# Attention groups of small matmul tiles set apart by whole products, two homes for two value tiles, another order for gates and exponentials

## What is computed

```
mod = (silu(c) @ wmod).reshape(2, 6, 1, 256); sa, ca, ga, sb, cb, gb = mod parts
h = layernorm(x) * (1 + ca) + sa
x = x + ga * gated_linear_attention(h)      # 16 heads of 16, chunks of 64 tokens
h = layernorm(x) * (1 + cb) + sb
x = x + gb * moe(h)                         # 8 experts, best 2 of them, width 176; a shared one, width 704

# attention, for each chunk: G = cumsum(log_sigmoid(h Wg1 Wg2 + bg2) / 16)
qg = Q * scale * exp(G);  o_inter = qg @ S
A  = tril((Q * exp(G - G0) * scale) @ (K * exp(G0 - G)).T);  o_intra = A @ V
S  = S * exp(Glast) + (K * exp(Glast - G)).T @ V
o  = rms_norm(o) * norm_w * silu(h Wgate);  out = o @ Wo
```

## Time and profile before

| | us |
|---|---|
| runs | 387.04, 387.41, 384.47 |
| median | 387.04 |
| profiled execution | 386.04 |
| its span | 384.2 |
| slot 1 (first gate product to first gate product) | 40.6 to 75.0 |
| slot 2 | 75.0 to 115.6 |
| slot 3 (to the first scores of slot 4) | 115.6 to 148.5 |
| slot 4, to the end of its mean squares | 148.5 to 174.0 |
| rest of the shared expert, sorting | 174 to 257 |
| expert tiles, combination | 257 to 384 |

### The profile page before, as it was taken

The page is one execution under the profiler, slowest core; times in us unless marked ns, Lnnn a source line. Parts: engine busy times, 40 slices in busy tenths (PEclk is TensorE's granted clock), DMA queues, the critical chain, the costliest instruction groups (busy, mean ns, idle before and its releaser), DMA issues.

```text
span 384.2 us, 9939 instructions
## 1 busy us (share of the span) xinstructions
PE 359.4 (94%) x3837; PEld 224.8 (59%) x3838; DVE 239.4 (62%) x578; ACT 144.4 (38%) x303; POOL 146.2 (38%) x252
## 2 busy tenths in 40 slices
PE   2989989997989899699999999999999999999996
PEld 2445655674556556554864564576666666666464
DVE  3068767796778878945286483236555555555386
ACT  3395718642846350335023311113333333332110
POOL 7504203500240062005544046540667777675300
PEclk9999999998999999999999999999999999999999
DMA  7960300000000000039931045242233333311296
GB/s 251 309 201 2 114 3 3 2 5 3 1 2 3 3 2 3 4 114 333 292 101 62 1 113 136 90 140 57 83 112 100 108 102 98 99 56 43 83 352 229
DMA packets 29901, 36.66 MB, mean 95 GB/s; under 512 B 4567, under 2 KB 26530, under 8 KB 29860
## 3 DMA queue, kind: packets, MB, share of 16 engines
q1 hardware_dynamic: 26452, 27.58, 23.9%
q0 software_dynamic: 3408, 8.51, 6.5%
HBM read 23.31 MB, written 13.68 MB: 96 GB/s over the span
## 4 chain that ended last, share of the span: by engine, by line
PE 85%; ACT 6%; DVE 4%; issue 3%; DMA 1%; SPq 0%; DVEq 0%; ACTq 0%
PE at_ps L1815 13%; PE work L1445 10%; PE at_ps L1445 8%; PE work L1494 6%; PE at_ps L1460 6%; PE work L1838 4%; PE work L1460 3%; PE work L1840 3%; PE work L1681 2%; PE work L1631 2%; PE at_ps L1494 2%; PE at_ps L1799 2%; PE at_ps L1528 2%; PE at_ps L1681 2%; PE o_even L1584 1%
## 5 line engine op out<-in xcount | busy, mean ns | idle before, releaser
L656 POOL DMA_INDIRECT ys_tokens<-er_pos,goal_u x39 | 41.8, 1073 | 33.8 <-DVE er_pos L1368 25.6
L1815 PE MATMUL at_ps<-arena 128*128 x156 | 54.5, 472 | 0.0
L627 POOL DMA_INDIRECT xs_sorted<-h2tok,pos_u x32 | 31.8, 993 | 36.9 <-DVE pos_u L992 18.6
L585 POOL TENSOR_TENSOR sq<-sq,sg 128x512 f32<-128x512 f32 x8 | 10.0, 1271 | 92.6 <-issue 92.6
L1815 PEld LDWEIGHTS at_ps<-arena 128*128 128x128 f32 x156 | 26.6, 190 | 14.9 <-issue 6.6
L898 ACT ACTIVATE arena<-at_ps 128x176 f32<-128x176 f32 x39 | 12.4, 317 | 58.8 <-PE at_ps L1815 58.8
L1368 DVE SCALAR_TENSOR_TENSOR er_pos<-work,goal,sq 128x256 f32<-128x256 f32 x39 | 17.2, 480 | 22.0 <-PE work L1845 21.0
L1445 PE MATMUL work<-h2T,sup_sb 128*128 128x512 f32 x56 | 25.7, 598 | 0.0
L1348 DVE TENSOR_TENSOR arena<-at_ps,arena 128x176 f32<-128x176 f32 x39 | 13.3, 341 | 18.4 <-ACT arena L898 15.9
L1195 DVE COPY_PREDICATED arena<-causal,at_ps 128x512 f32<-128x512 uint32 x32 | 20.5, 719 | 5.8 <-PE at_ps L1528 5.8
L1460 PE MATMUL at_ps<-sdn_sb,hs 128*128 128x256 f32 x100 | 22.1, 380 | 0.0
(11 more groups left out here) (281 smaller groups left out, 815.6 us busy)
## 6 DMA issues: line engine op xcount, KB each, us to landing
h2tok<-xs_sorted SPq DMA_DIRECT2D x40, 131.5 KB, 2.1
arena<-ys_tokens SPq DMA_DIRECT2D x8, 512.0 KB, 7.8
arena<-in_e_up SPq DMA_DIRECT2D x8, 352.0 KB, 5.5
x_sb<-in_x SPq DMA_DIRECT2D x4, 512.0 KB, 6.9
out_rows<-x_sb SPq DMA_DIRECT2D x16, 128.0 KB, 4.2
sup_sb<-in_s_up SPq DMA_DIRECT2D x2, 640.0 KB, 4.7
xs_sorted<-state SPq DMA_DIRECT2D x2, 526.0 KB, 15.2
xs_sorted<-state SPq DMA_DIRECT2D x8, 131.5 KB, 3.8
```

The lines of the kernel that those rows point to most:

```text
L627: g.indirect_dma_start(out=xs_dram, out_offset=bass.IndirectOffsetOnAxis(ap=pos_u[:, k, t:t + 1], axis=0), in_=h2tok[:, t, :], in_offset=N ...
L656: g.indirect_dma_start(out=ys_dram, out_offset=bass.IndirectOffsetOnAxis(ap=goal_u[:, i:i + 1], axis=0), in_=yout[:, q % 2, u, :], in_offs ...
L1815: ins = t_.matmul(at_ps[2 + u % 2][:, 0:2 * FE], xT[:, u % 2, k * P:(k + 1) * P], eup[:, bass.ds(e, 1), k, :].rearrange("p a n -> p (a n)" ...
```

## The change

TensorE, slots 1 to 3: `values(s, 0)` moves up between `scores_first` and `from_state`; K of half 0 between `from_state` and `scores_second`; the first of the two h2 transposes between `scores_second` and the first `from_chunk`; K of half 1 between the two `from_chunk`, with a wait for the mask that frees its bank; the second transpose, `mean_squares` and then `router` come behind the second `from_chunk`, and `logits_by_token` between the two query products. In slot 4 the shared part "half" stands in front of `scores_second`, and "second" in front of the second `from_chunk`.

The value tiles 0 and 1 of odd blocks get a second home, `vpad_odd` (zeroed once on GpSimd); ScalarE no longer waits for `from_chunk` ahead of `evac_v(s, 0)`. The masks are applied in the order of banks 2, 3, 0, 1 (`MASK_ORDER`). VectorE runs `log_gate(s, 0)` ahead of the masks and the x statistics ahead of the key evacuations. ScalarE takes er_neg out of `gate_exps` (`gate_neg`), one half behind `evac_v`, the other behind the first transpose's evacuation; `rstd_of(1)` goes behind the silu of G, and the squares ahead of the second transpose's evacuation, er_pos and the router's.

```diff
...
-BANKS = {("G", 0): 0, ("G", 1): 1, ("V", 0): 0, ("HT", 0): 1, ("HT", 1): 0, ("K", 0): 1, ("RT", 0): 0, ("RX", 0): 0, ("K", 1): 2,
+BANKS = {("G", 0): 0, ("G", 1): 1, ("V", 0): 0, ("HT", 0): 0, ("HT", 1): 0, ("K", 0): 1, ("RT", 0): 0, ("RX", 0): 0, ("K", 1): 2,
          ("Q", 0): 3, ("Q", 1): 1, ("V", 1): 0, ("KT", 0): 2, ("KT", 1): 3, ("XT", 0): 1, ("XT", 1): 0, ("WO", 0): 2,
...
+MASK_ORDER = (2, 3, 0, 1)
...
         put("V", s, 0)
+        put("K", s, 0)
         if h >= 0:
             put("HT", h, 0)
+        put("K", s, 1)
+        if h >= 0:
             put("HT", h, 1)
-        put("K", s, 0)
+            put("RT", h, 0)
+        put("Q", s, 0)
         if h >= 0:
-            put("RT", h, 0)
-        for kind, j in (("K", 1), ("Q", 0), ("Q", 1), ("V", 1), ("KT", 0), ("KT", 1)):
+            put("RX", h, 0)
+        for kind, j in (("Q", 1), ("V", 1), ("KT", 0), ("KT", 1)):
             put(kind, s, j)
-            if (kind, j) == ("K", 1) and h >= 0:
-                put("RX", h, 0)
         if s + 1 < NBLK:
...
     fill(NBLK, "gates")
+    fill(NBLK, "half")
     turn(("HT", NBLK - 2, 0), ("HT", NBLK - 2, 1), ("RT", NBLK - 2, 0))
-    fill(NBLK, "half")
+    fill(NBLK, "second")
     turn(("RX", NBLK - 2, 0), ("RK", 0, 0))
-    fill(NBLK, "second")
     ring.append(4)
...
         atm = part(2 * NPAIR * 512).rearrange("p (a j n) -> p a j n", a=2, j=NPAIR)
+        vpad_odd = part(2 * KC * NPAIR * 64).rearrange("p (t r w) -> p t r w", t=2, r=KC * NPAIR)
         wmod_sb = hs[:, :, :].rearrange("p f n -> p (f n)").rearrange("p (k n) -> p k n", k=KC)
...
+        def v_rows(s, t):
+            return vpad_odd[:, t] if t < 2 and s % 2 else vpad[:, t]
...
                             ALU.mult).then_inc(const_pool, 1)
+            steps.did(g.memset(vpad_odd, 0.0))
+            steps.sync()
             g.memset(vpad, 0.0).then_inc(zero_ready, 1)
...
-            def evac_h2T(b):
-                for k in range(KC):
+            def evac_h2T(b, ks=range(KC)):
+                for k in ks:
                     wait_unit(act, ("HT", b, k))
...
                 for t in range(2):
-                    ins = a.activation(free_dims(vpad[:, 2 * jj + t, 0, 0:1], [[64, KC * NPAIR], [48, 2], [1, HEAD]]),
+                    ins = a.activation(free_dims(v_rows(s, 2 * jj + t)[:, 0, 0:1], [[64, KC * NPAIR], [48, 2], [1, HEAD]]),
                                        bank(("V", s, jj))[:, t * HID:(t + 1) * HID]
...
+            def gate_neg(s, gr):
+                act.wait_ge(r_ready, 2 * s + gr + 1)
+                if s >= 1 and gr == 0:
+                    act.wait_ge(qeo_ready, 4 * s)
+                a.activation(er_neg[:, gr, :], gk[:, gr, :], ACT.Exp, scale=-1.0 / GATE_NORM).then_inc(neg_ready, 1)
             def gate_exps(s):
-                for gr in range(KC):
-                    act.wait_ge(r_ready, 2 * s + gr + 1)
-                    if s >= 1 and gr == 0:
-                        act.wait_ge(qeo_ready, 4 * s)
-                    a.activation(er_neg[:, gr, :], gk[:, gr, :], ACT.Exp, scale=-1.0 / GATE_NORM).then_inc(neg_ready, 1)
                 for gr in range(KC):
...
                     softplus(s)
-                if h >= 0:
+                else:
                     rstd_of(1, h + 1, h)
...
                 if s < NBLK:
-                    if b >= 0:
-                        act.wait_ge(set_used, 2 * b + 1)
-                    else:
+                    if h >= 0:
+                        rstd_of(1, h + 1, h)
+                    if b < 0:
                         act.wait_ge(zero_ready, 5)
                     evac_v(s, 0)
-                if h >= 0:
+                    gate_neg(s, 0)
+                    if h >= 0:
+                        evac_h2T(h, (0,))
+                    gate_neg(s, 1)
+                    if b >= 0:
+                        out_squares(b)
+                    if h >= 0:
+                        evac_h2T(h, (1,))
+                    gate_exps(s)
+                    if h >= 0:
+                        evac_router(h)
+                else:
+                    fill(s, "half")
                     evac_h2T(h)
                     evac_router(h)
-                fill(s, "half")
-                if b >= 0:
+                    fill(s, "second")
                     out_squares(b)
-                fill(s, "second")
                 if fills:
                     exp_ln_tables()
-                if s < NBLK:
-                    gate_exps(s)
                 if s + 1 < NBLK:
...
                     dve.wait_ge(set_used, n - 1)
-                for j in range(NPAIR):
+                for j in MASK_ORDER:
                     dve.wait_ge(at_full, NPAIR * n + j + 1)
...
                     ln_stats(1, h * TPB)
+                if s < NBLK:
+                    log_gate(s, 0)
                 if b >= 0:
...
                     mask_scores(2 * b)
+                fill(s, "gates")
                 if h >= 0:
                     h2_rows(h)
-                fill(s, "gates")
+                fill(s, "half")
                 if b >= 0:
                     mask_scores(2 * b + 1)
-                if s < NBLK:
-                    log_gate(s, 0)
-                else:
+                if s == NBLK:
                     steps.did(v.tensor_copy(iota_f[:, :], iota_i[:, :]))
...
                     pick_experts(dve, v, steps, 0)
-                fill(s, "half")
+                fill(s, "second")
                 if s < NBLK:
...
                     copy_ranks(dve, v, 0, bank(("RK", 0, 0)))
-                fill(s, "second")
                 if s == NBLK:
...
                     token_weights(dve, v, steps, 0)
+                if s + 1 < NBLK:
+                    dve.wait_ge(ld_x[s + 1], 16)
+                    ln_stats(0, (s + 1) * TPB)
                 if s < NBLK:
...
                         v.tensor_tensor(kh[:, gr, :], bank(("K", s, gr))[:, :], er_neg[:, gr, :], ALU.mult).then_inc(kh_ready, 1)
-                if s + 1 < NBLK:
-                    dve.wait_ge(ld_x[s + 1], 16)
-                    ln_stats(0, (s + 1) * TPB)
                 if h >= 0 and s < NBLK:
...
                         if b >= 1 and q == 0:
-                            pe.wait_ge(atm_ready, NPAIR * (2 * b - 1) + j + 1)
+                            pe.wait_ge(atm_ready, NPAIR * (2 * b - 1) + MASK_ORDER.index(j) + 1)
                         score(2 * b, q, j)
...
                         if q == 0:
-                            pe.wait_ge(atm_ready, NPAIR * 2 * b + j + 1)
+                            pe.wait_ge(atm_ready, NPAIR * 2 * b + MASK_ORDER.index(j) + 1)
                         score(2 * b + 1, q, j)
...
                                     ins = t_.matmul(o_ps[e][32 * j:32 * j + 32, o_reg(gr, t)],
-                                                    vpad[ks, t, gr * NPAIR + j, 32 * h:32 * h + 32],
+                                                    v_rows(b, t)[ks, gr * NPAIR + j, 32 * h:32 * h + 32],
                                                     atm[ks, n % 2, j, q:q + CHUNK],
...
-            def transpose_h2(b):
+            def transpose_h2(b, ks=range(KC)):
                 pe.wait_ge(h2tok_ready, b + 1)
-                for k in range(KC):
+                for k in ks:
                     o = begin(("HT", b, k))
...
                             ins = t_.matmul(at_ps[e][r, reg], ktok[ks, t, gr, r],
-                                            free_dims(vpad[ks, t, gr * NPAIR + j, 0:1], [[48, 2], [1, HEAD]]),
+                                            free_dims(v_rows(s, t)[ks, gr * NPAIR + j, 0:1], [[48, 2], [1, HEAD]]),
                                             start=True, stop=True)
...
                     scores_first(b)
+                if s < NBLK:
+                    if s == 0:
+                        pe.wait_ge(ld_wv, 16)
+                    values(s, 0)
                 fill(s, "gates")
...
                     if s == 0:
-                        pe.wait_ge(ld_wv, 16)
-                    values(s, 0)
+                        pe.wait_ge(ld_wk, 16)
+                    project(("K", s, 0), wk_sb, 0, hT)
+                fill(s, "half")
                 if b >= 0:
                     scores_second(b)
+                if h >= 0:
+                    transpose_h2(h, range(KC) if s == NBLK else (0,))
+                if b >= 0:
                     from_chunk(b, 2 * b)
-                if h >= 0:
-                    transpose_h2(h)
-                if s < NBLK:
-                    if s == 0:
-                        pe.wait_ge(ld_wk, 16)
-                    project(("K", s, 0), wk_sb, 0, hT)
-                if h >= 0:
+                if s == NBLK:
+                    router(h)
+                    fill(s, "second")
+                else:
+                    if b >= 0:
+                        pe.wait_ge(atm_ready, NPAIR * (2 * b + 1) + MASK_ORDER.index(2) + 1)
+                    project(("K", s, 1), wk_sb, 1, hT)
+                if b >= 0:
```

(30 more changed lines are left out.)

## The result

The changed kernel takes 383.42 us (median of 10 runs, 381.91 to 384.59); the kernel before, on the same chip, 387.23 us (10 runs, 384.47 to 388.11). The ratio is 0.9914, 95% interval 0.9889 to 0.9938: 3.3 us or 0.9% faster. That is within 1% and inside the forecast range, but by only 0.2 us (its lower end is 383.2); the forecast itself was 0.7 us faster, 386.3. The profiled execution took 383.4 us (span 381.6), where the one of before took 386.04.

The account below looks back on a forecast made before the run. TensorE, busy 94% of the span, bounds the kernel, with slot stalls from instruction fetch. Slots 1 to 4 sum +1.4 - 1.8 + 1.4 - 1.7 = -0.7 us, giving 386.3 us; range 383.2 to 389.8.

Parts of the forecast that it names:

- Slot 1: +1.4 us: gate-bank wait +0.45, stall where `scores_second` and `from_chunk` still touch 1.8 for 1.45, mean squares waiting +0.6.
- Slot 3: +1.4 us: h2 transpose waits 1.1 us for VectorE; output product waits 1.7 us for yT instead of 0.81.
- What is late next: Slot 3, VectorE: `evac_logits` and `top_two` (1.25 us) lose their cover ahead of the query evacuations; `gated_out` ends 144.7, was 143.34.
- Slot 4: -1.7 us: `from_chunk` stall of 1.40 and router wait of 0.7 go; SiLU bank wait of 0.25 comes.
- 3.4 to 3.9 us: TensorE's instruction fetch: a block of 256 instructions comes this long after the border before it was passed.
- Slot 2: -1.8 us, middle of -2.6 (stall, half clock and yT wait go) and -1.0 (1.6 us of stall return).
- the walk: TensorE's queue followed with old-trace pitches, each group waiting for its needs; slot 2's query product at 96.65, y at 105.5.
- the prediction's signs: Signs to look for in the trace, among them output products of slots 2 and 3 waiting 1.2 to 1.8 us for yT.
- (A): Rival: fetch problem really goes, slots 1 and 2 lose their stalls; -3.3 us, 383.7 us; chance 0.18.
- (B): Rival: waits for h2 bring the clock down in slots 2 and 3, stall in full; +2.7, 389.8 us; chance 0.14.
- (C): Rival: tile-shape switches cost 0.4 us instead of 0.1 at 8 islands; +2.4 over forecast, 388.7 us; chance 0.05.
- (D): Rival: every 256 instructions have a border, stalls only change place, sum zero; 387.0 us; chance 0.63 together with the forecast.

Follow-up runs that it names:

- run with the rows first: Changed kernel with VectorE taking the first log gate behind the expert-input rows instead of ahead of the masks in slots 2 and 3: 384.44 us, ratio 0.9936.
- shift of 136: Changed kernel with 136 idle instructions, as 34 small products, at the head of TensorE's program: 381.15 us, ratio 0.9853; made of waits instead, 391.01 us.
- first shifted run: Kernel before with 200 more instructions, waits on a long-set semaphore, at the head of TensorE's program: 405.93 us, ratio 1.0493.
- cheap shift of 168: Kernel before with 168 instructions, as 42 small identity products, at the head of TensorE's program: 388.40 us, ratio 1.0033.

## Why the prediction was right or wrong

**Slot 1, right.** Forecast +1.4, measured +1.8. The border at 1217 stayed inside the pair that still touches, as the prediction said, with 1.70 us (forecast 1.8); the value product waits 0.5 us for the gate (0.45), the mean squares 0.7 us for the squares (0.6). Not foreseen: 0.44 us at the next border, which is the difference.

```profile
54.77 0.26 PE L1605 MATMUL o_odd<-arena 64*32 64x64 f32 x3 [1.70 <-issue]
```

**Slot 3, right.** Forecast +1.4, measured +1.0. The rows of the second norm are late by 0.9 us (1.1). "What is late next" is in the trace as walked; the rows of the changed kernel that answer to the earlier trace rows are

```profile
136.92 0.20 DVE L1168 COPY logits<-work 128x36 f32<-128x36 f32 x1 [4.80 <-PE work L1638]
138.12 1.39 DVE L1329 SCALAR_TENSOR_TENSOR arena<-at_ps,qsel,er_pos 128x512 f32<-128x512 f32 x2
...
141.76 0.68 DVE L1235 TENSOR_TENSOR yT<-o_odd,sq 128x512 f32<-128x512 f32 x1
```

yT ends 28.7 us after the slot's first gate product, where the forecast had 144.7 - 115.6 = 29.1, and the output product waits 1.3 us (1.7). What the prediction could not see is that moving the top two out of this chain gives 0.9 us at most, with intervals that overlap.

**Slot 4, right.** Forecast -1.7, measured -1.9: the 1.40 us stall and the router's wait of 0.7 went, 0.6 us in the state products and 0.5 us for the SiLU (0.25) are left. The "3.4 to 3.9 us" from border to block does not hold for the stall in the state products: it was 5.9 us in before and is 6.0 now. Five instructions behind the border (148.86 us) TensorE's sequencer waits from 149.76 us for the state that GpSimd writes,

```profile
150.69 0.67 POOL L623 TENSOR_TENSOR arena<-state,tmask 128x64 f32<-128x64 f32 x1
```

and the packet starts at 152.56 us, 1.2 us after the state is there; in before it is 1.2 us as well. The shared part's products run over this wait, so it shows in no list of waits, only in the stall behind. That this wait is what held the packet is read from the times and was not tested alone.

**Slot 2, the step that failed.** The prediction let 0.8 us of the old stall stand, as the middle between none and 1.6, because "the fetch of the block ... starts only when the sequencer is some 30 instructions past a border, and the wait for h2 stands in front of that point". All queues together moved this in 86 to 90 us, in forty slices of 0.1, with the wait's end beside it:

```profile
GB/s 0 0 0 0 0 0 0 0 0 0 0 0 0 0 0 0 0 0 0 0 0 164 0 0 0 0 0 0 0 0 0 0 0 0 0 0 0 0 0 0
```

```profile
88.85 0.66 PE L1623 MATMUL work<-ident,h2tok 128*128 128x128 f32 x4 [0.99 <-DVE h2tok L1226]
...
90.89 1.56 PE L1515 MATMUL at_ps<-hT,wk_sb 128*128 128x512 f32 x3
```

The block's packet starts at 88.1 to 88.2 us, 0.7 us ahead of the end of the wait (88.85). The border (instruction 2497) stands 11 instructions ahead of the waiting transpose, and 11 were enough. So this wait did not block the fetch; it covered it. The prediction's rule was not wrong altogether, as slot 4 shows, where a wait 3 to 5 instructions behind the border goes with a late packet; what failed is its 30 instructions. The chunk product behind runs through the border at 2753 without a stop, and the key product starts at 90.89. The run with the rows first is the other half of the proof: without the wait, 0.56 us of stall. This is worth the 0.8 us down to the forecast's own end of -2.6. Beyond that end lies another 0.5 us. By the walk the first query product starts 21.6 us after the slot's first gate product and y stands at 30.5; the trace has 21.8 and 30.0. So it lies behind the query product, where one small operation of VectorE was long before and is short now:

```profile
105.27 1.29 DVE L1163 TENSOR_SCALAR sgate<-sgate_e 128x4 f32<-128x4 f32 x1 [0.98 <-ACT sgate_e L732]
```

```profile
104.52 0.15 DVE L1184 TENSOR_SCALAR sgate<-sgate_e 128x4 f32<-128x4 f32 x1
```

Why its length varies (0.81 us in the run with the top two moved), no run shows. For the same reason the output product of slot 2 waits only 0.45 us for yT, where the prediction's signs had 1.2 to 1.8.

**Up to slot 1, 0.6 us.** The forecast had nothing. The gate logits' four products in the loading stage took 1.70 us in before and 1.20 in the profiled run after. Slot 1 starts at 39.4 to 41.2 us in the profiled runs of the changed order and its variants that nothing shifts, and at 40.6 in before. I take the 0.6 us for chance and no gain.

**Rivals.** (A) gave 383.7 us, and its number came out nearly, which is closer than the forecast's 386.3; its conditions came out only in half: slot 2 lost its stall, slot 1 did not, and the waits for h2 stayed. With a shift of 136 slot 1 loses it too, and the time falls by the further 2.4 us. (B), the waits bring the clock down: the clock is 1.00 through the slots of the profiled run of the changed kernel, and no wait of 0.9 to 1.3 us lowered it. (C), dearer changes of shape: a value product between two small groups

```profile
118.39 2.00 PE L1652 MATMUL work<-wv_sb,hT 128*128 128x256 f32 x8
120.31 0.43 PE L1589 MATMUL o_odd<-arena 32*32 32x64 f32 x16
```

takes 1.92 us from its start to the next as in the earlier trace rows (the 1.72 us that the prediction sets against it are the third line of the earlier trace rows, not the last), so 0.1 us a change stands, and the drain that the Trainium skill ("TensorEngine Tiling (Array Packing)", Key Properties) speaks of costs no more than that here. (D), the stalls only change place: three places of the borders in before hold 5.8 to 7.8 us of stalls, three of the changed kernel and its variants 0.2 to 3.7. The sum of gains and waits is not zero either: 3.3 us. Out.

**What stays open.** Which part carries the gain is narrowed down, not shown. Order of the masks and place of the value product: nothing measurable. Place of the first key product: a loss of 2.6 us against the better one. Log gate and exponentials: 0.9 us, inside the intervals. The clock: some 1.4 us, by the three runs of before that kept it, as a consequence of the stall of slot 2 that went. What is left are the second key product and the two h2 transposes, one ahead of each chunk product and one behind, with the second home that lets them stand there; the stalls of 2.22 and 1.40 us that went stood in the chunk products. It was not tried alone, because without the second home ScalarE's evacuation would wait for a chunk product that stands behind its own transposes.

## What to carry to other kernels

Where an idle time before a product is put down to nothing and the products around it are many and small, count the engine's instructions: if the gaps are 256 apart, the program is the limit, and a large product inside each 256 instructions may hide up to its own length. Shift the program by a hundred cheap instructions to test that, and look at the gaps and at the granted clock of every run, not at the time alone. A wait that goes may uncover such a gap, and a gap that goes may uncover a wait: read what each of the two was covering before you price its removal.

## What the runs showed of the hardware

- A block of 256 instructions moves as one packet of 16 KB. In all fourteen traces, up to 185 us, a block was never in use less than 1.20 us after its packet had ended, and at the 49 stalls it was 1.20 to 1.53 us. The packets of the stalled blocks took 0.9 to 1.4 us. From one border to the next with a stall before it, 2.1 to 4.1 us passed in dense code, 5.9 to 6.6 us in slot 4's state products, and 9.8 us once, with a load on another queue. The Trainium skill ("Runtime: NRT & Kernel Launch", Instruction fetch mechanics) has the block of 256 instructions and says that the fetch is hidden by the pace of issue; these traces bear out the block and not the hiding, with 6.2 us of stalls in before.
- A wait on a semaphore that is long set cost TensorE 0.11 us an instruction (200 of them in a row in the first shifted run). Instructions of small products cost 0.006 to 0.009 us each in the slots (256 in 1.5 us, 128 in 1.1 us).
- In the slots the granted clock fell to 0.50 in three of the fourteen traces: in before at 89.6 us for 3.4 us, 1.1 us after a stall of 2.22 us; with 200 inserted at 64.1 us for 6.8 us, 1.9 us into a stall of 2.93 us; and in the cheap shift of 168 at 107.0 us for 3.4 us, 0.4 us after a wait of 1.67 us. Other stalls of 1.3 to 1.7 us left it at 1.00. The product at half clock took 3.23 us for 1.9 in the first of these and 3.39 for 2.0 in the last.
